# The low half of the split tokens read from PSUM at the beginning of the turn, in the last stage of a four-stage sequence model

## The reference, cut to what matters

```python
x = attn_layer(shift_tokens(x), Wqkv[i], q_scale[i], k_scale[i], Wo[i]) + x
x = ffn_layer(shift_tokens(x), ln_g[i], ln_b[i], W1[i], b1[i], W2[i], b2[i]) + x

def shift_tokens(t):                     # the first 64 channels stay,
    a, s = jnp.split(t, 2, -1)           # the last 64 come from the token before
    s = jnp.pad(s, ((0, 0), (1, 0), (0, 0)))[:, :-1]
    return jnp.concatenate([a, s], -1)

def attn_layer(x, Wqkv, qs, ksc, Wo):    # 16 heads of 64
    q, k, v = jnp.split(x @ Wqkv, 3, -1)
    q, k = l2norm(q) * qs, l2norm(k) * ksc
    q, k = rotary(q), rotary(k)
    # softmax(8 q k) v in windows of 32 tokens, each with the window before it
    return out @ Wo

def ffn_layer(x, ...):
    a, gate = jnp.split(layernorm(x) @ W1 + b1, 2, -1)
    return a * gelu(gate) @ W2 + b2
```

## Time and profile before

| | |
|---|---|
| median of three runs | 4238.78 us |
| lowest and highest run | 4233.77 and 4241.29 us |
| the profiled execution | 4246.35 us |
| span of its profile, first to last instruction | 4244.5 us |
| stage D within the span | from about 1320 us to the end |
| busy over the span | PE 92%, DVE 83%, ACT 62%, POOL 56% |
| granted clock over the span | 0.964 |

### The profile page before, as it was taken

The page is one execution under the profiler, slowest core; times in us unless marked ns, Lnnn a source line. Parts: engine busy times, 40 slices in busy tenths (PEclk is TensorE's granted clock), DMA queues, the critical chain, the costliest instruction groups (busy, mean ns, idle before and its releaser), DMA issues.

```text
span 4244.5 us, 120128 instructions
## 1 busy us (share of the span) xinstructions
PE 3910.8 (92%) x48128; PEld 2747.8 (65%) x48128; DVE 3529.0 (83%) x5537; ACT 2638.6 (62%) x5550; POOL 2381.6 (56%) x2045
## 2 busy tenths in 40 slices
PE   3457999999995999999999999999999999999998
PEld 1225776767764676667766676667766676667666
DVE  6875556777776899989998899989998899989897
ACT  3543336666664666666667666666666666666665
POOL 0111001000003787878888788878888787878785
PEclk7678999999997999999999999999999999999999
DMA  3000000000001333333332333333332333333332
GB/s 104 0 0 1 1 1 1 1 0 0 0 1 40 76 90 82 69 76 88 78 78 65 79 88 81 70 75 94 73 81 62 81 87 81 71 73 72 91 77 65
DMA packets 264482, 238.94 MB, mean 56 GB/s; under 512 B 31524, under 2 KB 260136, under 8 KB 263208
## 3 DMA queue, kind: packets, MB, share of 16 engines
q1 hardware_dynamic: 263976, 231.82, 23.5%
HBM read 26.20 MB, written 4.19 MB: 7 GB/s over the span
## 4 chain that ended last, share of the span: by engine, by line
PE 73%; DVE 12%; ACT 7%; issue 3%; SPq 2%; POOL 1%; DMA 1%; DVEq 0%; ACTq 0%; POOLq 0%
PE bank L1977 14%; PE bank L1910 13%; PE bank L1995 8%; PE bank L1950 7%; PE bank L2037 5%; PE bank L854 5%; ACT arena L1129 3%; PE bank L2050 2%; PE bank L1943 2%; DVE arena L1016 2%; PE bank L1921 2%; DVE arena L1026 2%; PE bank L1254 1%; SPq L2151 1%; PE bank L1245 1%
## 5 line engine op out<-in xcount | busy, mean ns | idle before, releaser
L1448 DVE TENSOR_TENSOR arena<-bank,tab 128x1024 f32<-128x1024 f32 x768 | 935.5, 1219 | 193.0 <-ACT arena L1680 138.8
L1835 POOL TENSOR_TENSOR arena<-arena 128x512 f32<-128x512 f32 x768 | 1010.7, 1332 | 49.6 <-DMA arena<-arena 44.9
L1680 ACT ACTIVATE arena<-bank 128x512 f32<-128x512 f32 x768 | 457.9, 596 | 538.9 <-PE bank L1910 530.1
L1977 PE MATMUL bank<-m_vo,arena 128*32 128x512 f32 x6144 | 757.9, 599 | 17.4 <-DVE arena L1541 11.1
L1910 PE MATMUL bank<-x_split,wqk_split 128*128 128x256 f32 x4608 | 720.7, 299 | 34.9 <-DVE arena L1448 21.0
L1910 PEld LDWEIGHTS bank<-x_split,wqk_split 128*128 128x128 f32 x4608 | 605.6, 192 | 184.3 <-issue 93.9
L1843 POOL TENSOR_TENSOR arena<-arena 128x256 f32<-128x256 f32 x768 | 558.6, 739 | 159.4 <-ACT arena L1680 158.7
L1704 ACT ACTIVATE arena<-bank 128x512 f32<-128x512 f32 x768 | 456.8, 596 | 186.9 <-PE bank L1977 184.2
L1852 POOL TENSOR_TENSOR arena<-arena 128x1024 f32<-128x1024 f32 x192 | 372.4, 1940 | 263.2 <-DVE arena L1496 263.2
L1187 POOL TENSOR_TENSOR x_all<-x_all,arena 128x256 f32<-128x256 f32 x16 | 11.6, 727 | 836.5 <-DVE arena L1008 836.5
L1858 POOL TENSOR_TENSOR arena<-arena 128x1024 f32<-128x1024 f32 x192 | 373.5, 1946 | 127.0 <-DVE arena L1509 126.7
(11 more groups left out here) (258 smaller groups left out, 7159.4 us busy)
## 6 DMA issues: line engine op xcount, KB each, us to landing
arena<-arena SPq DMA_DIRECT2D x1536, 128.0 KB, 2.5
wqk_stage<-in_wqk SPq DMA_DIRECT2D x6, 1024.0 KB, 8.6
out_x<-x_all SPq DMA_DIRECT2D x7, 512.0 KB, 6.0
wvt<-in_wvt SPq DMA_DIRECT2D x6, 512.0 KB, 4.4
wo<-in_wo SPq DMA_DIRECT2D x6, 512.0 KB, 5.5
arena<-in_wbh SPq DMA_DIRECT2D x1, 2048.0 KB, 9.7
w<-in_w SPq DMA_DIRECT2D x6, 341.0 KB, 5.9
wqk_stage<-out_x SPq DMA_DIRECT2D x2, 512.0 KB, 5.0
```

The costliest lines, as they stand in the source:

```text
L1448: nc.vector.tensor_tensor(d_t[c % KS].rearrange("p k h t -> p k (h t)"), bank[c % 2][:, :].unsqueeze(1).to_broadcast([P, 2, 2 * T]), tab[: ...
L1680: nc.scalar.activation(d_sq[i % 4].rearrange("p h t -> p (h t)"), bank[c % 2][:, :], ACT.Square).then_inc(s_sq, 1)
L1835: nc.gpsimd.tensor_tensor(d_rot[i // 4][:, i % 4, :, :], t[:, :, 0, :], t[:, :, 1, :], ALU.add).then_inc(s_ad, 1)
L1977: last = nc.tensor.matmul(bank[U_BANK[w]][g * WIN:(g + 1) * WIN, :], d_xt[n % 3][:, w * WIN:(w + 1) * WIN], m_vo[:, 4 * g:4 * g + 4, :].re ...
```

## The change

`split_low_tokens` takes the tokens from bank 6 instead of `d_xt`, in two operations: partitions 0 to 63 as they stand, and partitions 64 to 127 one token to the right. It is called second in DVE's turn, right after `turn_probabilities(f - 3, 1)`, instead of eleventh. Column 0 of the low half is zeroed once at the start of the stage. DVE gets a second wait (that the projection of unit n - 2 is over), and PE's `attention` waits for `s_split` too before it writes into bank 6.

```diff
-        ZEROS = 7
+        ZEROS = 8
...
             def split_low_tokens(n):
                 if not here(n):
                     return
                 dve.wait_ge(s_xh, n + 1)
-                nc.vector.tensor_tensor(x_split[:, n % 2, 1, :], d_xt[n % 3], x_split[:, n % 2, 0, :].bitcast(F32), ALU.subtract)\
-                    .then_inc(s_split, 1)
+                at_least(dve, s_proj, CHUNKS * (n - 1))
+                first, second, now = slice(0, C // 2), slice(C // 2, C), n % 2
+                nc.vector.tensor_tensor(x_split[first, now, 1, :], bank[6][first, 0:T],
+                                        x_split[first, now, 0, :].bitcast(F32), ALU.subtract)
+                nc.vector.tensor_tensor(x_split[second, now, 1, 1:], bank[6][second, 0:T - 1],
+                                        x_split[second, now, 0, 1:].bitcast(F32), ALU.subtract).then_inc(s_split, 1)
...
                 nc.vector.memset(v, 0.0).then_inc(s_zero, 1)
+            nc.vector.memset(x_split[:, :, 1, 0:1].bitcast(F32), 0.0).then_inc(s_zero, 1)
...
             for f in range(TURNS_D):
                 turn_probabilities(f - 3, 1)
+                split_low_tokens(f)
                 rotary_products(f - 1, 3)
...
                 softmax_maximum(f - 2, 1)
-                split_low_tokens(f)
                 ffn_gate(f - 4, 2)
...
                 if h == 0:
                     pe.wait_ge(s_xt, min(n + 4, TOTAL))
+                    pe.wait_ge(s_split, min(n + 4, TOTAL))
```

## The result

| | before | after |
|---|---|---|
| median of 20 runs each, us | 4239.56 | 4248.24 |
| lowest and highest, us | 4233.77 to 4245.89 | 4243.36 to 4252.13 |
| after / before, 95% interval | | 1.0020 [1.0013, 1.0027] |
| profiled execution, its span, us | 4246.35, 4244.5 | 4248.23, 4246.5 |

A forecast was written before the change was run, and what follows sets the result against it. PE's own work was taken to bound the kernel at 29.20 us a turn. Layer boundaries +4.7, fill -1.0 and memset +0.1 gave +3.8 us on the median 4238.78, or 4242.6 us, range 4231 to 4252.

The forecast's parts named there:

- What bounds the kernel: Steady turns of stage D: PE's own work sets the 29.20 us; the idle time "until L1436" is no real wait.
- Both faster rivals: Wait on L1436 real, 81 us saved, 4158 (2%); or DVE the true bound, 46 us saved, 4193 (2%).
- The old L1436 goes: Middle of each turn: frees about 1.28 us of DVE and 0.4 of POOL, worth nothing to the end time.
- Two operations at the beginning: Start of DVE's turn, ahead of product L1448: the pair takes 0.80 us, between 0.56 and 0.84.
- The held start: DVE's pair: moving to partition 64 and back holds each next instruction until earlier ones finish; sum 0.80 us or more.
- Where there is no room: First two turns of a layer, ten in all: the product ends 0.47 us too late, costing PE 4.7 us.
- The deadline of 4.24: Latest harmless end of product L1448, 4.24 us into the turn, before PE's projection chunk 5; PE loses any excess.
- The fill: Second turn of the stage: the projection no longer waits for L1436, so about 1.0 us is won.
- The sum: Whole kernel: +4.7 - 1.0 + 0.1 = +3.8 us on the median 4238.78, giving 4242.6 us.
- The range: Whole kernel: 4231 to 4252 us; the high end was 4246, stretched to nearly reach the milder slow case.
- the milder slow case: Pair of 1.1 us: product ends at 4.33 in ordinary turns, 5.01 in ten; 4253 us; 8% with the severe form.
- The slower rival: Product L1448: POOL blocks the pair, deadline missed every turn, 88 us lost, 4327; 8% together with a milder form.

The follow-up runs named there:

- the memset: Kernel before plus a memset of 832 spare-buffer columns ahead of rotary product 3 in turn 1 only; 4242.56 us against 4240.56, ratio 1.0005.
- the second measurement: The changed kernel, file unchanged, measured again against the kernel before: 4247.92 us against 4241.28, ratio 1.0016 [1.0007, 1.0025].
- The doubled pair: Changed kernel with two more such subtractions ahead of the two, each waited for; 4308.69 us, ratio to before 1.0159.

## Why the prediction was right or wrong

*What bounds the kernel.* Right. The ordinary turn stayed at 29.20 us although DVE got busier, and the idle time "until L1436" was no wait: the same 0.84 us stand there after the change (the load L1915 above), put down to issue. Both faster rivals fall with it.

*The old L1436 goes.* The worth for the end was right at nothing but for the third turns (-1.5 us), which I had not looked at. The reason that I gave was wrong in part: DVE did not gain 1.28 us in the middle of the turn. I took the blocking as L1436's own, where it belongs to whichever operation with two SBUF inputs comes while POOL is reading; L1462 stood next in line. DVE's busy time rose by 31 us over the run (3529.0 to 3560.1), where I had it lower.

*Two operations at the beginning.* Right in size: 0.80 us taken, 0.84 measured; product at 2.80 and 4.03 forecast for an ordinary turn, 2.76 and 3.99 measured. The held start, left open, was the true one.

*Where there is no room.* Right: 10 x 0.47 = 4.7 forecast, 5 x (0.39 + 0.41) = 4.0 measured. The deadline of 4.24 held in three kernels: 0.66, 0.42 and 0.20 us past it cost 0.64, 0.39 to 0.41 and 0.15 to 0.17.

*The fill.* This step failed. "About 1.0 us is won" and the split "moved past seven products, maxima and gates delays each by 0.7 us at most, and all but the product above have more room than that". That holds for the seven in the steady turn only. In the fill's turn 1 PE waited 5.21 us for this very product; the row was in the trace, and I had read the second wait of the fill but not the turn as a whole. Of the 1.0 us, 0.5 came, since L1926 itself ran at the lower clock. In place of -1.0 the fill brought +3.7 and +4.2 us in two traces. That a delay of this product is enough for a loss there is shown by the memset (+2.1 and +2.4 us against the two traces with the fill of before); how the loss divides between the 0.88 us and the clock is not settled, and single traces of the fill differ by some 2 us for reasons I don't know.

*The sum.* With 4.0 - 1.5 + 3.7 = 6.2 in place of 3.8 the trace accounts for most of 8.7 us, and lies within the interval (5.5 to 11.4) and by the second measurement's 6.6. The 2 us or so between the trace's sum and the first measurement are not explained.

*The range.* The bounds of my terms gave 4246 at the most. The measured 4248.2 is above that, and it lies in the stated range only because I had stretched the high end to 4252 for the milder slow case, which did not come. That was luck, not understanding.

*The slower rival*, a pair missing the deadline in every turn, did not come: the pair took 0.84 us, and it needs 1.1. The doubled pair shows that its price was reckoned in the right way, since every ordinary turn then lost what went past 4.24.

## What to carry to other kernels

Before an operation is moved, go through every kind of turn, the fill and the layer boundaries too, and ask which of them already waits for what will stand behind it; the steady turn gave 0 us here, and twelve other turns gave all of the loss that the traces show. Look for a deadline on PE's side and count in full what goes past it. An operation that a neighbour engine blocks is not rid of by being taken out, if the next in line has the same kind of inputs.

## What the hardware showed that was not expected

- The blocking by POOL moved to the next operation: L1466 took 1221 ns in the median where L1462 took 457, and DVE's busy time rose by 31 us, with no effect on PE.
- Two DVE operations that start at other partitions than the one before cost 0.85 us, two that all start at 0 cost 0.64, at nearly the same durations of their own.
- In the fill, a delay of 0.75 us on DVE went with 3.4 us on the turn against one trace and 1.2 against another, and with 2.4 and 2.1 us on three turns. PE's granted clock in the turn was 0.50 (1.2 GHz) where it had been 0.62 and 0.56; PE was busy for 13.7 of 25.3 us without the delay and 15.9 of 28.6 with it.
